# Attention stacks by six transfers a group, the first sequence's constants on GpSimd, and its scores behind 18 row maxima

## What is computed

```python
y = (x - mu) * jax.lax.rsqrt(var + LN_EPS) * gamma1 + beta1
...
h = jnp.einsum('becd,fd->becf', xg, w1) + b1
...
x_mlp, x_qkv = (h[..., :MLP_HID], h[..., MLP_HID:])
q, k, v = (qkv[0], qkv[1], qkv[2])
scale = HEAD_DIM ** (-0.5)
attn = jax.nn.softmax(jnp.einsum('bhqd,bhkd->bhqk', q, k) * scale, axis=-1)
x_attn = jnp.einsum('bhqk,bhkd->bhqd', attn, v)
...
x_mlp = jax.nn.gelu(x_mlp, approximate=False)
y2 = jnp.concatenate([x_mlp, x_attn], axis=-1)
```

## Time and profile before

| | us |
|---|---|
| median of three runs | 2194.19 |
| lowest and highest | 2193.48 to 2196.16 |
| profiled execution, its own time | 2192.55 |
| span of its profile | 2190.8 |
| TensorE busy | 1974.5 (90%) |
| VectorE busy | 1137.2 (52%) |
| ScalarE busy | 750.8 (34%) |
| GpSimd busy | 428.5 (20%) |
| mean granted clock of TensorE | 0.936 |

### The profile page before, as it was taken

How to read it: one execution, slowest core, us unless ns; L and a number is a source line. 1 busy time by engine, 2 the same in 40 slices (tenths; PEclk the granted TensorE clock), 3 DMA queues, 4 the chain that set the end, 5 groups by cost and what they waited for, 6 DMA issues and landing times. The chain is left out here.

```text
span 2190.8 us, 27883 instructions
## 1 busy us (share of the span) xinstructions
PE 1974.5 (90%) x10040; PEld 1243.3 (57%) x10048; DVE 1137.2 (52%) x2687; ACT 750.8 (34%) x1251; POOL 428.5 (20%) x526
## 2 busy tenths in 40 slices
PE   4996618999999999679999999699999999999997
PEld 2343513444444444446666665465567888888886
DVE  5798577666666756156677676337411222222221
ACT  1434002555455545355555554121111111111111
POOL 5200100121012201211111111110371222322232
PEclk9988558999999999979999999789999999999999
DMA  2600002121111111000000000200123221222221
GB/s 64 229 34 0 0 13 89 47 61 52 51 37 58 51 51 30 13 14 6 6 6 6 6 6 6 97 2 1 48 77 95 67 59 30 67 60 61 67 36 19
DMA packets 68618, 94.30 MB, mean 43 GB/s; under 512 B 15354, under 2 KB 57630, under 8 KB 66209
## 3 DMA queue, kind: packets, MB, share of 16 engines
q1 hardware_dynamic: 52354, 76.76, 10.9%
q0 software_dynamic: 16128, 15.76, 4.1%
HBM read 54.53 MB, written 39.47 MB: 43 GB/s over the span
## 5 line engine op out<-in xcount | busy, mean ns | idle before, releaser
L972 DVE TENSOR_REDUCE row_max<-c_ps_m 128x1 f32<-128x512 f32 x384 | 252.6, 686 | 115.9 <-PE c_ps_m L1130 110.5
L1308 ACT ACTIVATE e<-c_ps_s 128x512 f32<-128x512 f32 x384 | 216.6, 596 | 222.1 <-PE c_ps_s L1146 221.3
L2593 DVE TENSOR_TENSOR e_f<-e_ps_u,e_gate 128x512 f32<-128x512 f32 x120 | 83.0, 691 | 271.2 <-ACT e_gate L2875 178.7
L2394 POOL DMA_INDIRECT out<-m_o,m_row_of x80 | 125.7, 1571 | 281.5 <-issue 251.6
L2810 PE MATMUL e_ps_o<-m_w,e_f 128*128 128x192 f32 x960 | 162.6, 326 | 0.9 <-DVE e_f L2593 0.9
L1130 PE MATMUL c_ps_m<-c_kT,qT 96*128 96x512 bf16 x384 | 150.3, 398 | 11.0 <-DVE row_max L972 10.9
L2810 PEld LDWEIGHTS e_ps_o<-m_w,e_f 128*128 128x128 f32 x960 | 158.1, 190 | 3.3 <-DVE e_f L2593 1.3
L1146 PE MATMUL c_ps_s<-qT,c_kT 97*128 97x512 bf16 x384 | 145.5, 389 | 12.3 <-ACT e L1308 5.0
L2875 ACT ACTIVATE e_gate<-e_ps_g 128x512 f32<-128x512 f32 x120 | 71.6, 597 | 242.3 <-PE e_ps_g L2784 162.3
L2778 PE MATMUL e_ps_g<-m_xT,m_w 128*128 128x256 f32 x480 | 129.6, 392 | 1.0 <-DVE h L2425 1.0
L2778 PE MATMUL e_ps_u<-m_xT,m_w 128*128 128x256 f32 x480 | 123.2, 379 | 0.0
(11 more groups left out here) (430 smaller groups left out, 3766.2 us busy)
## 6 DMA issues: line engine op xcount, KB each, us to landing
dealt<-x SPq DMA_DIRECT2D x8, 1290.0 KB, 15.1
m_x<-dealt SPq DMA_DIRECT2D x40, 258.0 KB, 2.7
spread<-parts SPq DMA_DIRECT2D x24, 384.0 KB, 2.4
qT<-spread SPq DMA_DIRECT2D x144, 64.0 KB, 2.4
c_kT<-spread SPq DMA_DIRECT2D x144, 64.0 KB, 2.4
m_w<-in_w13e SPq DMA_DIRECT2D x8, 1152.0 KB, 5.3
m_w<-in_w2e SPq DMA_DIRECT2D x8, 576.0 KB, 6.4
out<-h SPq DMA_DIRECT2D x8, 384.0 KB, 4.5
```

The costliest lines, as they stand in the source:

```text
L972: dve.tensor_reduce(row_max[:, n // J, n % J:n % J + 1], ps_m[:, n % 2, :], AX_X, ALU.max)\
L1308: act.activation(e[:, n % LIVE_E, :], ps_s[:, n % 2, :], ACT.Exp, scale=QSCALE).then_inc(e_ready, 1)
L2394: pool.indirect_dma_start(out=out_rows, out_offset=bass.IndirectOffsetOnAxis(ap=row_of[:, n % 2, r:r + 1], axis=0), in_=o[:, n % 2, r, :], ...
```

## The change

Four things are done.

1. The weights' columns for q and k are laid out on the host so that the 64 rows of a group are dimension-major (row = dimension x 4 + head). The scratch in memory becomes [group][q or k][part][64 rows][512]: the four heads of a dimension lie in one run of 4096 bytes. `parts_to_scratch` writes it by two transfers (q half, k half) of 64 x 3 x 512 instead of one of 128 x 1536.
2. `stacks_from_scratch` reads six transfers a group instead of twelve: the query's part 0 into slots 0 to 2 by one transfer that reads it three times, part 1 into slots 3 and 4 by one that reads it twice, part 2 into slot 5; the key's parts 0 to 2 into slots 0 to 2, parts 0 and 1 into 3 and 4, part 0 into 5. The same six products come out.
3. The three fills go from VectorE to GpSimd, between its y of sequence 0 and of sequence 1; TensorE waits for them ahead of the first values.
4. In the first sequence TensorE runs two hidden tiles, then the other four ahead of maxima 0, 4, 8 and 12, then the maxima up to the 18th, the transpose, the values and the scores. `FIRST` = 18; the maxima 18 to 33 come two by two behind score steps 0 to 7, after which the order is that of before. VectorE copies the values behind the placing of the maxima.

```diff
+FIRST = GS + 2
+def maxima_of(t, n):
+    def done(m):
+        usual = LEAD + BETWEEN + sum(k not in NO_MAXIMA for k in range(m + 1))
+        return usual if t > 0 else min(usual, FIRST + 2 * (m + 1))
+    return range(done(n - 1), done(n))
...
-                sp.dma_start(spread[g], parts[:, g, :, :]).then_inc(parts_out[g], 16)
+                for w in range(2):
+                    sp.dma_start(spread[g, w].rearrange("s r n -> r s n"), parts[w * P // 2:(w + 1) * P // 2, g, :, :])\
+                      .then_inc(parts_out[g], 16)
...
+                q_at, k_at = (spread[g, w].rearrange("s (d i) n -> s d (i n)", d=HD) for w in range(2))
...
+                for part, (first, slots) in enumerate(((0, 3), (3, 2), (5, 1))):
+                    at = slice(first * HD, (first + slots) * HD)
+                    sp.dma_start(qT[at, heads, :], q_at[part:part + 1].broadcast_to([slots, HD, 4 * T])).then_inc(stack_in[g], 16)
+                    sp.dma_start(kT[at, heads, :], k_at[0:slots]).then_inc(stack_in[g], 16)
...
             finish_y(0)
+            pool.wait_ge(y_ready, 1)
+            pool.memset(kT[STACK:STACK + 1, :, :], 1.0).then_inc(ones_ready, 1)
+            pool.wait_ge(ones_ready, 1)
+            pool.memset(v[:, :, :, :, HD:HD + 1].rearrange("p u j h d -> p (u j) h d"), 1.0).then_inc(ones_ready, 1)
+            pool.memset(v[:, :, :, :, HD + 1:32].rearrange("p u j h d -> p (u j) h d"), 0.0).then_inc(ones_ready, 1)
             finish_y(1)
...
-            for m in range(FC1_TILES):
+            for m in range(2):
                 mlp_tile(0, m)
+            for n in range(FIRST):
+                if n % 4 == 0 and n < GS:
+                    mlp_tile(0, 2 + n // 4)
+                maxima(0, n)
+            max_transpose(0, 0)
+            pe.wait_ge(ones_ready, 3)
             for j in range(J):
                 values(0, j)
-            for n in range(LEAD + BETWEEN):
-                maxima(0, n)
-                if n == GS + 1:
-                    max_transpose(0, 0)
```

More of the change, by code:

```diff
@@ L729 @@
 STACK = PAIRS * HD
-QUERY_SLOTS = ((0, 1, 2), (3, 4), (5,))
-KEY_SLOTS = ((0, 3, 5), (1, 4), (2,))
-STACK_LOADS = 2 * PAIRS
+STACK_LOADS = 6
 LIVE_E = 8
@@ L741 @@
 BANKS = 3
-def maxima_of(n):
-    return [] if n in NO_MAXIMA else [LEAD + BETWEEN + n - sum(m < n for m in NO_MAXIMA)]
+FIRST = GS + 2
[4 more added lines that the diff above has]
+    return range(done(n - 1), done(n))
 def work_order(by_end=False):
@@ L770, in work_order @@
         if not prev:
-            order += [("v", t, j) for j in range(J)] + [("mx", t, 0)]
+            order += [("mx", t, 0)] + [("v", t, j) for j in range(J)]
         if ahead:
@@ L852, in parts_to_scratch @@
                     sp.wait_ge(stack_in[g], t * STACK_LOADS * 16)
-                sp.dma_start(spread[g], parts[:, g, :, :]).then_inc(parts_out[g], 16)
+                for w in range(2):
+                    sp.dma_start(spread[g, w].rearrange("s r n -> r s n"), parts[w * P // 2:(w + 1) * P // 2, g, :, :])\
+                      .then_inc(parts_out[g], 16)
             def stacks_from_scratch(t, g):
-                heads, q_at, k_at = slice(4 * g, 4 * g + 4), spread[g, 0:P // 2], spread[g, P // 2:P]
-                sp.wait_ge(parts_out[g], t * 16 + 16)
+                heads = slice(4 * g, 4 * g + 4)
+                q_at, k_at = (spread[g, w].rearrange("s (d i) n -> s d (i n)", d=HD) for w in range(2))
+                sp.wait_ge(parts_out[g], t * 32 + 32)
                 if t > 0:
                     sp.wait_ge(s_psum, (t - 1) * NS + (g + 1) * GS)
-                for s in range(3):
-                    for at in QUERY_SLOTS[s]:
-                        sp.dma_start(qT[at * HD:(at + 1) * HD, heads, :],
-                                     q_at[:, s, :].rearrange("(i d) n -> d i n", d=HD)).then_inc(stack_in[g], 16)
-                    for at in KEY_SLOTS[s]:
-                        sp.dma_start(kT[at * HD:(at + 1) * HD, heads, :],
-                                     k_at[:, s, :].rearrange("(i d) n -> d i n", d=HD)).then_inc(stack_in[g], 16)
+                for part, (first, slots) in enumerate(((0, 3), (3, 2), (5, 1))):
+                    at = slice(first * HD, (first + slots) * HD)
+                    sp.dma_start(qT[at, heads, :], q_at[part:part + 1].broadcast_to([slots, HD, 4 * T])).then_inc(stack_in[g], 16)
+                    sp.dma_start(kT[at, heads, :], k_at[0:slots]).then_inc(stack_in[g], 16)
             def maxima_to_queries(t, g):
@@ L950, in split_high @@
                 if t > 0:
-                    dve.wait_ge(parts_out[g], t * 16)
+                    dve.wait_ge(parts_out[g], t * 32)
                 dve.tensor_copy(hml[:, 0, :], qk)
@@ L1020, in turn @@
                 for n in range(NS):
-                    for to in maxima_of(n):
+                    for to in maxima_of(t, n):
                         if to < NS:
@@ L1066, in _ @@
             norm_apply(1)
-            for j in range(J):
-                v_copy(0, j)
-            for n in range(LEAD + BETWEEN):
+            for n in range(FIRST):
                 row_maximum(0, n)
@@ L1072, in _ @@
                     negate_maxima(0)
-                if n == GS + 1:
-                    place_maxima(0, 0)
+            place_maxima(0, 0)
+            for j in range(J):
+                v_copy(0, j)
             for t in range(B):
@@ L2948, in lay_out @@
     w1[CH, 1] = np.asarray(i["L0_ffn_b1"])
[L2949 to L2950 removed]
+    w1[:, :, MLP:MLP + 2 * C] = w1[:, :, MLP:MLP + 2 * C].reshape(CH + 1, 2, 2, G3, 4, HD)\
+                                                         .transpose(0, 1, 3, 2, 5, 4).reshape(CH + 1, 2, 2 * C)
     w2 = np.asarray(i["L0_ffn_w2"]).T
```

11 lines of the change are left out of this document (3 added, 8 removed).

## The result

The changed kernel took 2202.48 us (median of 14 runs, 2198.61 to 2215.84) beside 2194.39 us for the kernel before (14 runs, 2189.45 to 2198.91): ratio 1.0051, 95% interval 1.0035 to 1.0067. It is 8.1 us slower. The forecast was 2194.7, with a range up to 2198.5, so the prediction was wrong. Nearest to the result is its second rival (2200.9 us, chance 0.1).

A forecast was written before the change was run, and what follows sets the result against it. TensorE was taken to bound seven of eight sequences, so only the phase's start could gain. Terms -4.2 +4.4 -4.5 +4.8 gave +0.5 us, added to the 2194.19 median: 2194.7 us, range 2189.8 to 2198.5.

The forecast's parts named there:

- rival 2: Narrow transfers at 0.23 us a row hold the first engine 8.9 us a group; +6.7, 2200.9 us; chance 0.1.
- three signs named beforehand: Wrong if TensorE waits for stacks in later sequences, fills run past 332 us, or second placing moves over 3 us.
- end of placing to the turn's first reduction: First sequence: 2.65 us against 7.16 before, as the ten maxima no longer stand between; -4.5 us.
- The fills and the splits: Phase start: fills on GpSimd, estimated 6.3 us, cost nothing; first cast about 324.55, all three splits end 1.77 us earlier.
- How many engines: Stack loads: merged query transfers run on 3 and 2 engines, giving the first engine 39 rows a group.
- rival 1: All sixteen engines share the query transfers; maxima start at 335.7; -2.0, 2192.2 us (2190.0 to 2193.5); chance 0.2.
- The landing: Group 0's stacks: issued from 330.9, landed at 338.5, so first maxima start 4.2 us earlier after a 5.2 us stand.
- The clock: After TensorE's 5.2 us stand: 1.2 GHz makes the first tile cost 0.4 to 1.7 us more, taken as 1.2.
- The four values fit behind it: First sequence, after the maxima placing at 355.3: the values fit before scores start at 357.2.
- Later sequences: From sequence 1's first group, 1.3 us of room: cost nothing; 1.2 to 1.7 us once if rows take 0.23 us.
- The turn with ten maxima more: First reduction within the turn to second placing: 20 reductions instead of 10, 21.4 us against 16.6, +4.8.
- The tiles among the maxima: First sequence: a tile after every fourth maxima makes each group 3.76 us against 2.56, three times, +3.6 us.

The follow-up runs named there:

- filler: The changed kernel with ten extra matmuls (results unused) on TensorE just before the first maxima: 2208.99 us, ratio 1.0071; repeated as filler_2, ratio 1.0063.
- q_single: The changed kernel with its merged query transfers taken apart into six of 16 rows, key transfers still merged, nine a group: 2193.72 us, ratio 0.9996.
- held_back: The changed kernel with all transfers of groups 1 and 2 kept back in the first sequence until group 0's stacks have landed: ratio 1.0043.
- q_single_tiles_first_2: Second run of the changed kernel with single query transfers and all hidden tiles ahead of the first maxima: 2187.95 us, ratio 0.9972.
- old_order: The changed kernel with its six new transfers, but the first sequence in the order of the kernel before: 2200.3 us, ratio 1.0023.
- k_narrow: The changed kernel with four padding rows behind each part in the scratch, to make the key transfers narrow too: 2264.05 us, ratio 1.0309.

## Why the prediction was wrong, step by step

Times are those of the profiled execution in before's time. Two of the three signs named beforehand came: TensorE waited for stacks in a later sequence, and the second placing moved by 11.1 us (378.85 to 389.96). The fills were over long before 332 us.

The kernel of filler, traced twice, shows how far one execution can be trusted in these rows: its first placing ended 47.36 us after the phase's first row in one trace and 44.27 in the other, with one slow tile less.

| step | forecast | measured |
|---|---|---|
| first cast | 324.55 | 324.78 |
| SyncE at the stacks | 330.9 | 331.47 |
| first maxima matmul | 338.5 | 343.51 |
| from there to the end of placing | 16.8 | 20.02 |
| end of placing to the turn's first reduction | 2.65 | 5.13 |
| first reduction to the second placing's end | 21.4 | 21.30 |
| second placing ends | 379.35 | 389.96 |
| wait for stacks in sequence 1 | 0 | 2.00 |

- **The fills and the splits**: right. GpSimd's 5.21 us for 6144 elements was even a little less than my 6.3.
- **How many engines**: right, three and two; rival 1 fell. q_single, in which no query transfer is narrow, measured 2193.7, beside that rival's 2192.2 (to 2193.5), with three issues more for a group.
- **"At 27 GB/s 5.9 us ... The landing: 330.9, plus 1.5 us ... plus 5.9, plus 0.2"**: this step failed. The landing took 12.04 us where the term has 7.6. It was near in what it charged for a further row (0.14 to 0.20 us measured against 0.15) and wrong in the rest. Beside the bytes I counted 1.5 us for the first group's issue and completion, where about 4 us went, and I charged 0.2 us for the other groups' transfers, which cost 1.6 to 2.0 (held_back). Rival 2 came near in time by luck, by a reason that is not the measured one: it charged more for a row, 0.23 us.
- **"The clock ... so the first tile costs 0.4 to 1.7 us more; I take 1.2"**: failed. Two tiles ran at 1.2 GHz: +3.2 us up to placing. The stand was 9.94 us instead of 5.2, but that its length is the reason isn't shown: filler, with a stand of 1.56, had two slow tiles as well.
- **"The four values fit behind it"**: failed. The term put them at nothing; they took 5.38 us at 1.2 GHz, and the turn's first reduction came 2.5 us later than forecast. The late stacks are not the reason: the clock had been back at 1.00 and fell again in the short waits of the maxima for VectorE, and in q_single_tiles_first_2, which never stood, they took 5.30 us. Ahead of the maxima, where the kernel before and old_order have them, they take 2.77.
- Landing, tiles and values (5.0 + 3.2 + 2.5) make the 10.6 us by which the second placing missed its forecast in this execution.
- **"Later sequences ... Cost nothing"**: failed. I had written 1.2 to 1.7 us for the case of slow rows and left it out of the sum; the trace has 2.00, old_order 2.79 and filler_2 3.85. It is the same landing again: 8.2 us forecast (381.42 to 389.6), 10.31 measured. The earlier TensorE gets there, the longer it waits, so part of what is saved in the first stand is lost here.
- **The turn with ten maxima more**: right to 0.1 us (21.30). The clock stayed up through it.
- **The tiles among the maxima**: charged at +3.6 us in my sum and taken as given. q_single against q_single_tiles_first_2 (0.9996 against 0.9972) shows that it was the difference between no gain and a gain of 6 us over the kernel before, which the old order with these transfers has to the greater part too (0.9983).
- **The chances**: 0.1 for rival 2 was too little. The room at sequence 1 was only 1.3 us, and I took the rate of a lone transfer, seen over 35 us, for a group among others. Apart from rival 1, each uncertainty of the landing pointed to later.

## What to carry to other kernels

Merging transfers saves issues, but count the engines of the merged one: a repeat dimension on the reading side left three and two of sixteen, and the group lands with the engine that has most rows. Time a landing from a transfer of the same size in the same company, and charge the issue, the completion and the neighbours beside the bytes. If work is to be brought forward behind a transfer, place the independent work (here the four tiles) ahead of the waiting instruction and not behind it: the same work in the two orders differed by about 5 us (0.9996 against 0.9972). And follow the work that was put off: here it took back, by the second placing, the 4.6 us by which the scores had begun sooner than in the old order.

## What the runs showed of the hardware that was not expected

- TensorE's clock stayed at 1.2 GHz after the stand through 12 us with 10.97 of them busy (0.50 from 340 to 356). The earlier trace rows had such a stretch already (12.70 us with 10.84 busy at 0.51), beside one of 3.10 us; I took the short one for my forecast.
- The same stretch of work does not always bring the same clock. My rival 1 took 2.88 busy us of 4.00 as enough to lose it. In the kernel before, the same 2.88 of 4.00 are followed once by the slow clock and once, a sequence later, by the fast one:

```profile
447.20:451.20 4.00, 2.88 (x16) 0.77 (x16) 3.70 (x8) 2.25 (x4) 0.00 (x0) 0.98 0.27 91
451.20:455.20 4.00, 4.00 (x18) 2.17 (x11) 1.89 (x5) 1.11 (x3) 0.00 (x0) 0.59 0.57 159
...
519.60:523.60 4.00, 2.88 (x16) 0.77 (x16) 3.71 (x7) 2.28 (x4) 0.00 (x0) 1.00 0.28 94
523.60:527.60 4.00, 4.00 (x27) 2.85 (x20) 2.93 (x12) 2.17 (x4) 0.00 (x0) 1.00 0.45 126
```

  From one placing of maxima to the next these two take 18.8 and 17.2 us. Of the six such places in later sequences the trace of before has four at 18.7 or more, that of the changed kernel two at 18.5 or more; by an estimate from these, 1.6 us at each of six places could make most of the 10 us over which one kernel's times spread.
- Padding of four rows in the scratch, which changed no byte moved, took a kernel from 1.005 to 1.031 times the time before. The DMA share in k_narrow is 0.23 from 340 to 342, where the changed kernel has 0.75, and 0.19 to 0.20 from 342 to 346; that the key transfers of three and two slots then ran on three and two engines is inferred from that and from the landing.
- The kernel before took 2194 us on two chips and 2237 us on two others, with a spread there of about 20 us against 10 us.
